# Dense block 0 made in memory of its own, beside the end of the last attention pass, with the routing exponential behind it

## The chip, the cores and the metric
The kernel runs on one core of one Trainium2 chip. Its time is the device time of one execution in microseconds (us), given as the median of several runs. The engines are TensorE (PE, matmuls; PEld are its weight loads), VectorE (DVE), ScalarE (ACT), GpSimd (POOL) and SyncE (SP, which here only issues transfers). Each runs its own list of instructions in order and waits on semaphores for the others.

## The reference
Input are 16 x 256 = 4096 tokens of 512 values. First comes a layer of attention over the 16 heads of each token, then a feed-forward layer:

```python
x = x + xattn(layernorm(x), ctx, ctx, ...)        # scores between the 16 heads of one token
x = x + ffn(layernorm(x), ...)

def ffn(z):                                       # E = 8 experts, F = 352, shared width 704
    scores = softmax(z @ gate_weight.T)
    topk_w, topk_idx = top_k(scores, 2)
    y = sum over the 2 experts: w * (silu(z @ gate.T) * (z @ up.T)) @ down.T
    sgu = z @ shared_gate_up.T
    return y + (silu(sgu[:, :704]) * sgu[:, 704:]) @ shared_down.T
```

## The kernel before
**Passes.** The tokens go in 16 blocks of 256. Attention is a loop of passes: pass i scores and attends block i, projects block i + 1 ahead, and does the rest of block i - 1 behind it (output projection `project_out`, residual and statistics `add_attended`, normalised rows `z`, their transposes `turn_z`, the routing logits `route` and `turn_logits`). Pass 15 (`NB - 1`) is written out and projects nothing ahead. What is left of block 15 is done behind it, the steps called with `NB`.

**Dense blocks.** The shared (dense) feed-forward part works on the same 16 blocks, which the text calls dense blocks 0 to 15. `gate_up(i, b, fs)` makes the gate and up products of six chunks f of 128 hidden units (the last has 64), one PSUM bank for each; 24 matmuls a chunk, 12 for the last. Every product is made of three fp16 matmuls, of a high and a low part. Then ScalarE makes the SiLU (`gate`), VectorE multiplies by the up half (`gate_times_up`), ScalarE rounds to the high part (`hidden_high`), VectorE makes the low part (`hidden_low`), and PE multiplies by the down weights (`down`, 36 matmuls: chunks 0 to 4 for both halves of the tokens, then chunk 5 for both). VectorE adds the result to `base` (`add_shared`). Each chunk passes between the engines four times. `sh_out` counts what VectorE finishes: six chunks and two halves, so 8 (`SH_STEPS`) a block.

**Around block 0.** Its weights are cut into high and low parts in pass 15: `shared_high` (ACT) and `shared_low` (DVE), four pieces each, once `find_scale` has a power of two for them. PE runs `gate_up(0, ...)` in three places between the last steps of block 15, since its banks are free by then. Before the first of them it waits for all four `shared_low` and for the two scales `wsd_scaled` and `wd_scaled`, because their input lies in a bank that `gate_up` writes. `gate_act` (the SiLUs, three buffers in turn) and `sh_t` (the hidden parts) lie in memory that the passes use until their last stores to HBM have landed. So ScalarE and VectorE turn to block 0 only when `x1`, `z` and the columns `zt` of block 15 are stored: VectorE waits for that, makes the routing maximum and difference (L1670, L1671), ScalarE the routing exponential (L1225), and only then `gate(0, 0)` (L1236) follows on ScalarE.

**SyncE's list.** It issues in this order: the stores of block 15, after their landing the eight loads of the routed experts' gate and up weights (`load_expert`, L668), a store that clears the slot table (L676), the columns of dense block 2 (`next_columns`, L607), the store of base 0 (L662), after that store has landed the load of base 2 (L611), the columns of block 3, and so on; the down weights of the experts (L679) stand behind the columns of block 4.

**Routing.** Behind `add_shared(0)` VectorE picks the top two experts of all tokens (L1725 to L1742), PE ranks them between two parts of `gate_up(1, ...)`, and behind `add_shared(1)` VectorE works out the slots (L1750 to L1770). In blocks 2 and 3 it also finds the largest expert weight in 16 reductions (`largest`, L1705). GpSimd scatters the token numbers to their slots beside blocks 2 to 8. Then come the routed experts, 71 slots of 128 rows, and the last six dense blocks with the sum of all parts.

The waits of PE that order `down(0)`:

```python
for step in ("LT", "Z0", "Z1"):
    wait_drained(pe, step, NB)
down(0, 0)
```

## Time and profile before

| | us |
|---|---|
| median of 3 runs | 1449.7 (1448.55 to 1450.1) |
| the profiled execution, device time | 1446.31 |
| its span in the profile | 1444.6 |
| PE busy in the span | 1340.1 (93%) |
| DVE busy | 884.4 (61%) |
| ACT busy | 674.4 (47%) |
| mean granted clock of PE | 0.98 |

The time runs about 1.7 us over the span in the profiled execution. In a timeline a row is a group of like instructions: its start, its length, engine, line of the kernel, what it writes and reads, the count, and in brackets the idle time before it with what ended it. The clock that PE is granted has two levels, 1.00 (2.4 GHz) and 0.50 (1.2 GHz).

### The profile page before, as it was taken

To read this page: it belongs to the slowest core of one execution; us is meant where nothing else is said; L and a number is where in the kernel's file an instruction comes from. 1 tells how busy PE (TensorE), PEld (TensorE's weight loads), DVE (VectorE), ACT (ScalarE), POOL (GpSimd) and SP (SyncE) were. 2 spreads that over 40 slices of the span, in tenths; PEclk is the share of its full clock that TensorE was granted. 3 is DMA by queue.
4 is the path that set the end of the run, shared out by engine and by line. 5 is a ranking of instruction groups with operands and counts; after the bars stand their busy time and mean duration, and the time that the engine had idled before them with its cause. 6 is when DMAs were issued, how large, how long until landed. Compare 5 with 4: busy or idle time off the path is not lost.

```text
span 1444.6 us, 34230 instructions
## 1 busy us (share of the span) xinstructions
PE 1340.1 (93%) x11411; PEld 1005.0 (70%) x11412; DVE 884.4 (61%) x1952; ACT 674.4 (47%) x1500; POOL 372.7 (26%) x480
## 2 busy tenths in 40 slices
PE   4799999999999997788999999999999999999997
PEld 4688788888888885656767756666666666657675
DVE  6888888888888888667855532232232232224566
ACT  6276667777676776431444423333333333332121
POOL 4322222222222220004566011111111111104554
PEclk9899999999999998899999999999999999999999
DMA  5556766776767658497734622222222222227996
GB/s 197 134 141 190 198 196 185 204 204 199 189 185 202 185 138 270 129 350 134 113 53 83 148 95 81 80 86 80 81 85 82 80 86 81 81 72 235 315 312 225
DMA packets 212740, 223.20 MB, mean 155 GB/s; under 512 B 84693, under 2 KB 142109, under 8 KB 212334
## 3 DMA queue, kind: packets, MB, share of 16 engines
q1 hardware_dynamic: 193608, 178.62, 43.5%
q0 software_dynamic: 12880, 35.47, 8.1%
q10 hardware_dynamic: 6198, 8.40, 2.0%
q8 instruction: 32, 0.52, 0.2%
q14 instruction: 22, 0.18, 0.1%
HBM read 129.30 MB, written 67.96 MB: 137 GB/s over the span
## 4 chain that ended last, share of the span: by engine, by line
PE 80%; DVE 11%; issue 2%; ACT 2%; DMA 2%; SPq 1%; POOL 0%; DVEq 0%; POOLq 0%; ACTq 0%
PE psum_b L726 44%; PE psum_a L726 30%; PE psum_b L1016 2%; PE psum_b L1038 2%; DVE z_parts L1472 1%; DVE k_scale L1394 1%; DVE d_m L1705 1%; PE psum_b L752 1%; SPq L488 1%; DVE wdn L1791 1%; DMA heads<-in_wk_t 1%; DVE gate_act L1680 1%; ACT z_parts L1120 1%; DMA wgu_in<-base_rows 1%; PE psum_b L784 0%
## 5 line engine op out<-in xcount | busy, mean ns | idle before, releaser
L726 PE MATMUL psum_a<-wgu,zg_t 128*128 x1704 | 267.7, 314 | 2.1 <-DVE zg_t L1802 1.7
L726 PEld LDWEIGHTS psum_a<-wgu,zg_t 128*128 128x128 f16 x1704 | 166.1, 98 | 90.2 <-issue 10.3
L726 PE MATMUL psum_a<-zt_in,wsgu 128*128 128x256 f16 x1536 | 170.6, 273 | 1.0 <-ACT y_sb L1306 0.8
L2025 POOL DMA_INDIRECT zg<-z_rows,gather_ix x71 | 67.2, 946 | 402.9 <-DVE gather_ix L1798 395.8
L726 PEld LDWEIGHTS psum_a<-zt_in,wsgu 128*128 128x128 f16 x1536 | 148.8, 98 | 24.9 <-issue 6.5
L1807 DVE SCALAR_TENSOR_TENSOR silu<-psum_a,w_scale,silu 128x352 f32<-128x352 f32 x71 | 41.5, 584 | 191.1 <-ACT silu L1293 191.1
L726 PE MATMUL psum_b<-wdn,act_t 128*128 (+1 forms) x639 | 149.6, 379 | 1.6 <-DVE act_t L1814 1.6
L726 PE MATMUL psum_b<-wsdn,sh_t 128*128 128x512 f16 (+1 forms) x576 | 134.4, 388 | 14.9 <-DVE sh_t L1686 14.4
L1912 POOL TENSOR_SCALAR var_eps<-mv 128x1 f32<-128x1 f32 x64 | 28.4, 443 | 429.7 <-DVE mv L1371 289.9
L1293 ACT ACTIVATE silu<-psum_a,w_scale 128x352 f32<-128x352 f32 x71 | 39.4, 554 | 202.4 <-PE psum_a L726 202.4
L726 PEld LDWEIGHTS psum_b<-wsdn,sh_t 128*128 128x128 f16 (+1 forms) x576 | 54.6, 99 | 88.9 <-issue 18.3
L1084 ACT ACTIVATE at_raw<-psum_a 32x128 f32<-32x128 f32 x384 | 103.2, 269 | 28.0 <-PE psum_a L726 23.5
L726 PE MATMUL psum_b<-cx_t,wk 128*128 128x256 f32 x768 | 102.9, 292 | 12.8 <-DVE k_scale L1414 6.5
L1236 ACT ACTIVATE gate_act<-psum_a,ws_scale 128x256 f32<-128x256 f32 x64 | 30.0, 470 | 175.1 <-PE psum_a L726 174.6
L1813 DVE TENSOR_TENSOR act_t<-psum_b,act_t 128x256 f16<-128x256 f32 x71 | 30.2, 425 | 129.6 <-ACT act_t L1084 129.6
L726 PEld LDWEIGHTS psum_b<-cx_t,wk 128*128 128x128 f32 x768 | 96.7, 196 | 16.9 <-DVE k_scale L1414 6.6
L726 PEld LDWEIGHTS psum_b<-wdn,act_t 128*128 128x128 f16 (+1 forms) x639 | 62.4, 98 | 61.6 <-issue 1.9
L1084 ACT ACTIVATE spread_t<-paired 32x512 f32<-32x512 f32 x128 | 90.2, 705 | 31.8 <-DVE paired L1458 30.6
L726 PE MATMUL psum_b<-wo,at_t 128*128 128x512 f32 x384 | 100.3, 415 | 0.0
L726 PE MATMUL psum_b<-xn_t,wq 128*128 128x256 f32 x768 | 97.5, 287 | 0.0
L1306 ACT ACTIVATE y_sb<-psum_b,wd_scale 128x512 f32<-128x512 f32 x71 | 48.8, 688 | 102.1 <-PE psum_b L726 102.1
L726 PEld LDWEIGHTS psum_b<-xn_t,wq 128*128 128x128 f32 x768 | 94.3, 194 | 0.7
(247 smaller groups left out, 2346.8 us busy)
## 6 DMA issues: line engine op xcount, KB each, us to landing
expert_rows<-y_sb SPq DMA_DIRECT2D x71, 256.0 KB, 2.0
k_st<-k_parts SPq DMA_DIRECT2D x192, 64.0 KB, 2.0
q_st<-q_parts SPq DMA_DIRECT2D x180, 64.0 KB, 2.0
wgu_in<-in_wgu_t SPq DMA_DIRECT2D x8, 1408.0 KB, 16.5
x_sb<-in_x SPq DMA_DIRECT2D x16, 512.0 KB, 5.5
cx_in<-in_ctx_t SPq DMA_DIRECT2D x16, 512.0 KB, 8.8
x_res<-in_x SPq DMA_DIRECT2D x16, 512.0 KB, 6.3
value_rows<-heads SPq DMA_DIRECT2D x16, 512.0 KB, 3.3
```

Of the source, the lines that this page charges most:

```text
L488: sp.dma_start(dst[HD * n:HD * (n + 1), :, KC * l:KC * (l + 1), :].rearrange("p j h g -> p j (h g)"), parts[HD * l:HD * (l + 1), part].rea ...
L726: return nc.tensor.matmul(o, l, r, start=start, stop=stop)
L1016: last = nc.tensor.transpose(t_bank[:, kc * P:(kc + 1) * P], zg[:, b, kc * P:(kc + 1) * P], ident[:, :])
L1038: last = nc.tensor.transpose(a_bank[0:fn, f * P:(f + 1) * P], silu[:, b, f0:f0 + fn], ident[:, :])
L1084: return nc.scalar.activation(o, i_, ACT.Copy)
L1236: nc.scalar.activation(gate_act[at:at + fn, f % GB, :], sh_bank(f)[0:fn, 0:BT], ACT.Silu, scale=ws_scale[0:fn, 3:4]).then_inc(silu_ready, 1)
L1293: nc.scalar.activation(silu[:, b, :], psum_a[:, 2 * b * BANK:2 * b * BANK + F], ACT.Silu, scale=w_scale[:, 3:4]).then_inc(g_silu, 1)
L1306: nc.scalar.activation(y_sb[:, b, :], d_bank[:, :], ACT.Copy, scale=wd_scale[:, 5:6]).then_inc(d_out, 1)
L1807: V.scalar_tensor_tensor(out=silu[:, b, :], in0=psum_a[:, (2 * b + 1) * BANK:(2 * b + 1) * BANK + F], scalar=w_scale[:, 4:5], in1=silu[:, ...
L1813: V.tensor_tensor(act_t[:, b, LO, 0:2 * P], psum_b[1][:, 0:2 * P], act_t[:, b, HI, 0:2 * P], ALU.subtract)
L1912: link(G.tensor_scalar_add(var_eps[:, col:col + 1], mv[:, col, 1:2], EPS))
L2025: pool.indirect_dma_start(out=zg[:, b, :], out_offset=None, in_=z_d[:, :], in_offset=bass.IndirectOffsetOnAxis(ap=gather_ix[:, b:b + 1], a ...
```

## The change
- `gates_of_first` (three gate buffers) and `hidden_of_first` (all hidden parts of one block) are placed in `wdn_in`, slots 2 to 6, where the last expert's gate and up weights land later. `gates_and_hidden(i)` gives these for block 0 and `gate_act`, `sh_t` for all others.
- SyncE waits in front of the eighth expert load for `sh_out` 8, that is for the whole of dense block 0.
- ScalarE in pass 15: `weights_out(0)`, two `shared_high`, `weights_out(1)`, two `shared_high`, instead of four `shared_high` and then both `weights_out`.
- VectorE in pass 15: the scales `wsd_scale` and `wd_scale` are found behind the fourth `shared_low`, not ahead of the first.
- ScalarE and VectorE behind pass 15: the steps of block 0 are put between those of block 15, in an order written out by hand; the wait for the stores, the routing maximum, the difference and the exponential come behind them.

```diff
+        gates_of_first = wdn_in[:, 2:4, :].rearrange("p e d -> p (e d)")[:, 0:GB * BT].rearrange("p (f t) -> p f t", f=GB)
+        hidden_of_first = wdn_in[:, 4:7, :].rearrange("p e d -> p (e d)").bitcast(F16).rearrange("p (h f t) -> p h f t", h=2, f=len(FS_CH))
+
+        def gates_and_hidden(i):
+            return (gates_of_first, hidden_of_first) if isinstance(i, int) and i == 0 else (gate_act, sh_t)
@@ SyncE
             def load_expert(e):
+                if e == E - 1:
+                    sp.wait_ge(sh_out, SH_STEPS)
+                    settle(sp)
@@ ScalarE, body
                 if isinstance(i, int) and i == NB - 1:
+                    weights_out(0, i)
                     act.wait_ge(ws_loaded, 48)
                     act.wait_ge(ws_scaled, 1)
-                    shared_high(range(KC))
-                weights_out(0, i)
-                weights_out(1, i)
+                    shared_high(range(2))
+                    weights_out(1, i)
+                    shared_high(range(2, KC))
...
@@ ScalarE, behind body(NB - 1)
             attended_out(NB)
             down_weights_high()
+            gate(0, 0)
+            gate(0, 1)
+            hidden_high(0, 0)
+            hidden_high(0, 1)
+            gate(0, 2)
+            gate(0, 3)
             z_out(NB)
             z_high(NB, 1)
+            hidden_high(0, 2)
+            hidden_high(0, 3)
+            gate(0, 4)
+            hidden_high(0, 4)
+            gate(0, 5)
+            hidden_high(0, 5)
             act.wait_ge(r_shift, 1)
             nc.scalar.activation(d_s[:, :, :], d_s[:, :, :], ACT.Exp).then_inc(r_exp, 1)
-            for f in range(len(FS_CH)):
-                gate(0, f)
-                if f > 0:
-                    hidden_high(0, f - 1)
-            hidden_high(0, len(FS_CH) - 1)
             gates(1, lambda f: None)
@@ VectorE, body
                 if isinstance(i, int) and i == NB - 1:
-                    find_scale(wsd_scale, psum_b[0][:, P:2 * P])
...
-                    find_scale(wd_scale, psum_b[0][:, 2 * P:3 * P])
-                    dve.sem_inc(wd_scaled, 1)
                     shared_low(0)
                     shared_low(1)
...
                 if isinstance(i, int) and i == NB - 1:
                     shared_low(2)
                     shared_low(3)
+                    find_scale(wsd_scale, psum_b[0][:, P:2 * P])
...
+                    find_scale(wd_scale, psum_b[0][:, 2 * P:3 * P])
+                    dve.sem_inc(wd_scaled, 1)
                 if behind:
                     turned_logits_out(i)
@@ VectorE, behind body(NB - 1)
             normalise_out(NB)
+            for f in range(2):
+                gate_times_up(0, f)
+            for f in range(2):
+                hidden_low(0, f)
             z_low(NB, 0)
+            for f in range(2, 4):
+                gate_times_up(0, f)
             logits_out(NB)
             z_low(NB, 1)
+            for f in range(2, 4):
+                hidden_low(0, f)
             turned_logits_out(NB)
+            for f in range(4, 6):
+                gate_times_up(0, f)
+                hidden_low(0, f)
             wait_drained(dve, "LT", NB)
...
             V.tensor_tensor(d_s[:, :, :], tok_scores[:, :, :], d_m[:, :].unsqueeze(2).broadcast_to([P, NT, E]), ALU.subtract).then_inc(r_shift, 1)
-            shared_block(0, 0, 0, nothing)
+            dve.wait_ge(base_loaded[0], 16)
+            add_shared(0, 0)
             dve.wait_ge(r_exp, 1)
```

## Rows read from the trace of the kernel before

**Rows 1.** The page: busy time of each engine.

```profile
PE 1340.1 (93%) x11411; PEld 1005.0 (70%) x11412; DVE 884.4 (61%) x1952; ACT 674.4 (47%) x1500; POOL 372.7 (26%) x480
```

**Rows 2.** Stretches of 20 us: busy time of the engines, granted clock, DMA.

```profile
600.00:620.00 20.00, 12.67 (x110) 10.29 (x109) 7.90 (x19) 6.46 (x14) 2.96 (x12) 0.90 0.43 155
```

**Rows 3.** The chain that ended last, in order of time: start, length, what.

```profile
611.37 2.99 DMA z_columns<-z_parts
...
615.83 1.28 ACT L1236
...
617.63 0.49 DVE gate_act L1680
618.15 0.42 ACT sh_t L1084
618.60 0.44 DVE sh_t L1686
...
619.27 9.76 PE psum_b L726 x36
```

**Rows 4.** Timeline of the end of pass 15 and the first part of gate_up(0).

```profile
570.87 5.55 ACT L1137 ACTIVATE wsgu<-wsgu_in,ws_scale 128x1408 f16<-128x1408 f32 x4 [2.46 <-DMA wsgu_in<-in_wsgu_t]
...
576.33 5.40 ACT L1084 ACTIVATE spread_t<-paired 32x512 f32<-32x512 f32 x8
...
577.43 0.28 DVE L1463 TENSOR_REDUCE wsd_scale<-psum_b 128x1 f32<-128x128 f32 x1
...
579.89 3.28 DVE L1487 SCALAR_TENSOR_TENSOR wsgu<-wsgu_in,ws_scale,wsgu 128x1408 f16<-128x1408 f32 x2 [0.16 <-DVE wd_scale L1468]
...
583.83 1.08 PE L726 MATMUL psum_b<-z_t,wgate 128*32 128x256 f32 x8 [5.08 <-DVE z_parts L1472]
...
585.91 3.27 DVE L1487 SCALAR_TENSOR_TENSOR wsgu<-wsgu_in,ws_scale,wsgu 128x1408 f16<-128x1408 f32 x2
...
588.53 0.66 PE L726 MATMUL psum_b<-strip_sum,logits_t 128*128 128x8 f32 x4
...
589.44 5.40 PE L726 MATMUL psum_a<-zt_in,wsgu 128*128 128x256 f16 x48 [0.25 <-DVE wsgu L1487]
```

**Rows 5.** Timeline of block 15's last steps on VectorE.

```profile
603.88 0.55 DVE L1519 TENSOR_SCALAR z<-x,mv,rstd 128x512 f32<-128x512 f32 x1 [0.76 <-POOL rstd L1913]
...
611.98 0.17 DVE L1482 COPY tok_scores<-psum_b 128x16 f32<-128x16 f32 x1 [0.71 <-PE psum_b L726]
```

**Rows 6.** Stretches of 1 us, as in rows 2; the granted clock is third from last.

```profile
572.00:573.00 1.00, 0.27 (x2) 0.00 (x0) 0.90 (x4) 1.00 (x2) 0.79 (x2) 1.00 1.16 311
...
575.00:576.00 1.00, 0.00 (x0) 0.00 (x0) 0.85 (x3) 1.00 (x2) 0.07 (x1) 0.50 1.06 389
...
622.00:623.00 1.00, 1.00 (x4) 0.36 (x3) 0.63 (x2) 0.20 (x1) 0.00 (x0) 0.60 1.03 397
```

**Rows 7.** SyncE's timeline, and the time to landing of its L607 at 634.89.

```profile
614.49 16.94 SPq L668 DMA_DIRECT2D wgu_in<-in_wgu_t  x8
...
634.89 7.43 SPq L607 DMA_DIRECT2D zt_in<-z_columns  x1
...
DMA to landing us min/median/max: 13.5/13.5/13.5
```

**Rows 8.** Timeline: down(1) on PE; block 2's first product, and its last down matmuls.

```profile
643.62 8.04 PE L726 MATMUL psum_b<-wsdn,sh_t 128*128 128x512 f16 x36
...
660.14 0.48 DVE L1680 SCALAR_TENSOR_TENSOR gate_act<-psum_a,ws_scale,gate_act 128x256 f32<-128x256 f32 x1
...
673.72 7.26 PE L726 MATMUL psum_b<-wsdn,sh_t 128*128 128x512 f16 x24 [1.04 <-DVE sh_t L1686]
```

**Rows 9.** SyncE's columns of block 5, their time to landing, and block 5's start.

```profile
710.00 3.12 SPq L607 DMA_DIRECT2D zt_in<-z_columns  x1
...
DMA to landing us min/median/max: 12.8/12.8/12.8
...
729.03 10.65 PE L726 MATMUL psum_a<-zt_in,wsgu 128*128 128x256 f16 x96
```

More of the change, by code:

```diff
@@ L934, in down @@
                             for hp, wp in PARTS:
-                                last = mm(sh_bank(n + s), sh_t[0:fn, hp, f, s * P:(s + 1) * P], wsdn[0:fn, wp, f, :],
+                                last = mm(sh_bank(n + s), hidden[0:fn, hp, f, s * P:(s + 1) * P], wsdn[0:fn, wp, f, :],
                                           f == 0 and (hp, wp) == PARTS[0], f == n - 1 and (hp, wp) == PARTS[-1])
@@ L1169, in body @@
                 if isinstance(i, int) and i == NB - 1:
+                    weights_out(0, i)
                     act.wait_ge(ws_loaded, 48)
                     act.wait_ge(ws_scaled, 1)
-                    shared_high(range(KC))
-                weights_out(0, i)
-                weights_out(1, i)
+                    shared_high(range(2))
+                    weights_out(1, i)
+                    shared_high(range(2, KC))
+                else:
+                    weights_out(0, i)
+                    weights_out(1, i)
                 if behind:
@@ L1235, in gate @@
                 at = REST if f == LAST else 0
-                nc.scalar.activation(gate_act[at:at + fn, f % GB, :], sh_bank(f)[0:fn, 0:BT], ACT.Silu, scale=ws_scale[0:fn, 3:4]).then_inc(silu_ready, 1)
+                nc.scalar.activation(gates_and_hidden(i)[0][at:at + fn, f % GB, :], sh_bank(f)[0:fn, 0:BT], ACT.Silu, scale=ws_scale[0:fn, 3:4]).then_inc(silu_ready, 1)
             def hidden_high(i, f):
@@ L1240, in hidden_high @@
                 act.wait_ge(sh_raw, i * len(FS_CH) + (f + 1))
[L1241 removed]
+                gates, hidden = gates_and_hidden(i)
+                copy(hidden[0:fn, HI, f, :], gates[0:fn, f % GB, :]).then_inc(sh_high, 1)
             def gates(i, after):
@@ L1260, in weights_high16 @@
                                ACT.Copy, scale=w_scale[:, 2:3]).then_inc(w_high16, 1)
-            for f in range(len(FS_CH)):
-                gate(0, f)
-                if f > 0:
-                    hidden_high(0, f - 1)
-            hidden_high(0, len(FS_CH) - 1)
+            attended_out(NB)
+            down_weights_high()
+            gate(0, 0)
[4 more added lines that the diff above has]
+            gate(0, 3)
+            z_out(NB)
+            z_high(NB, 1)
+            hidden_high(0, 2)
[4 more added lines that the diff above has]
+            hidden_high(0, 5)
+            act.wait_ge(r_shift, 1)
+            nc.scalar.activation(d_s[:, :, :], d_s[:, :, :], ACT.Exp).then_inc(r_exp, 1)
             gates(1, lambda f: None)
@@ L1661, in _ @@
             normalise_out(NB)
-            z_low(NB, 0)
-            logits_out(NB)
-            z_low(NB, 1)
-            turned_logits_out(NB)
-            wait_drained(dve, "LT", NB)
-            dve.wait_ge(z_stored, 16 * (NB + 1))
-            dve.wait_ge(x1_stored, 16 * (NB + 1))
-            dve.wait_ge(zt_stored, 16 * NB)
-            link(V.tensor_reduce(out=d_m[:, :], in_=tok_scores[:, :, :], axis=X, op=ALU.max))
-            V.tensor_tensor(d_s[:, :, :], tok_scores[:, :, :], d_m[:, :].unsqueeze(2).broadcast_to([P, NT, E]), ALU.subtract).then_inc(r_shift, 1)
             def sh_bank(step):
@@ L1679, in gate_times_up @@
                 at, up = (REST, 0) if f == LAST else (0, BT)
-                V.scalar_tensor_tensor(out=gate_act[0:fn, f % GB, :], in0=sh_bank(f)[at:at + fn, up:up + BT], scalar=ws_scale[at:at + fn, 4:5],
-                                       in1=gate_act[at:at + fn, f % GB, :], op0=ALU.mult, op1=ALU.mult).then_inc(sh_raw, 1)
+                gates = gates_and_hidden(i)[0]
+                V.scalar_tensor_tensor(out=gates[0:fn, f % GB, :], in0=sh_bank(f)[at:at + fn, up:up + BT], scalar=ws_scale[at:at + fn, 4:5],
+                                       in1=gates[at:at + fn, f % GB, :], op0=ALU.mult, op1=ALU.mult).then_inc(sh_raw, 1)
             def hidden_low(i, f):
@@ L1721, in nothing @@
                 pass
-            shared_block(0, 0, 0, nothing)
+            for f in range(2):
+                gate_times_up(0, f)
+            for f in range(2):
+                hidden_low(0, f)
+            z_low(NB, 0)
+            for f in range(2, 4):
+                gate_times_up(0, f)
+            logits_out(NB)
+            z_low(NB, 1)
+            for f in range(2, 4):
+                hidden_low(0, f)
+            turned_logits_out(NB)
+            for f in range(4, 6):
+                gate_times_up(0, f)
+                hidden_low(0, f)
+            wait_drained(dve, "LT", NB)
+            dve.wait_ge(z_stored, 16 * (NB + 1))
+            dve.wait_ge(x1_stored, 16 * (NB + 1))
+            dve.wait_ge(zt_stored, 16 * NB)
+            link(V.tensor_reduce(out=d_m[:, :], in_=tok_scores[:, :, :], axis=X, op=ALU.max))
+            V.tensor_tensor(d_s[:, :, :], tok_scores[:, :, :], d_m[:, :].unsqueeze(2).broadcast_to([P, NT, E]), ALU.subtract).then_inc(r_shift, 1)
+            dve.wait_ge(base_loaded[0], 16)
+            add_shared(0, 0)
             dve.wait_ge(r_exp, 1)
```

15 lines of the change are left out of this document (5 added, 10 removed).

## The prediction

> **What bounds the kernel now.** The busy line of the page comes first: PE works 93% of the span [rows 1], so time can only be won where PE stands still or runs at its lower clock. The stretches show where: from 600 to 620 us PE is busy 12.67 of 20 us at a granted clock of 0.90 [rows 2]. The chain of waits says why. PE's last matmul there ends at 611.9, and `down(0)` begins at 619.27, behind a line of single steps: the store of the columns lands (611.37 + 2.99), VectorE makes the routing maximum and difference and ScalarE the exponential (together 1.3 us), ScalarE loads its SiLU table (1.28), then SiLU, product, high part and low part of chunk 0 [rows 3]. That is 7.3 us of idle PE. The clock falls in it, and the 36 matmuls of `down(0)` take 9.76 us, where the 36 of `down(1)` take 8.04 [rows 3, 8]. So 9.0 us are to be had at most, if nothing else comes late. The timelines then tell what does.
>
> **Pass 15: the first part of gate_up(0) starts 1.45 us later.** Four `shared_high` take 5.55 us and eight copies of `weights_out` 5.40; the order is new and the sum is not. ScalarE can begin with `weights_out(0)` at 570.2, when VectorE has turned the pairs, and not at 570.87 when the weights land, so it comes to the columns of z some 0.65 us earlier. VectorE, without the two scales, has its first two `shared_low` done at 580.8 and waits there for ScalarE. `z_low(0)`, which lets PE's `route` go at 583.83, moves up by 0.8, and so do the last two `shared_low`, from 589.18 to 588.35. But the two scales now stand behind these: from 577.43 to 579.89 they take 2.3 us with their handoff left out. PE waits for both, so `gate_up(0)` starts at 588.35 + 2.3 + 0.25 = 590.9 where it started at 589.44 [rows 4]. From there to 611.9 PE had no gap, so this 1.45 us passes through to all of PE's steps.
>
> **Behind pass 15: ScalarE and VectorE.** What is added ahead of `z_low` costs PE nothing as long as it fits. VectorE ends z at 604.43 + 1.45 = 605.9 [rows 5], makes two products (0.9 us), waits for ScalarE's high parts and ends two low parts at 607.8; each handoff is as in rows 3. ScalarE then makes two SiLUs (1.0) and comes to z's first transpose at 608.15, where PE gave it at 608.0. `z_low(0)` ends at 610.0, and PE reaches `route` only at 611.0, so 1.0 us is left over; without that cover each us on VectorE is a us on PE. The columns are issued at 612.8, 1.45 later than before. The last transposed logits are out at 612.15 + 1.45 = 613.6, and PE, which waits for nothing later, starts `down(0)` at 613.9. Chunks 0 to 3 are ready by then (low part 3 ends at 613.6), chunk 4 at 615.4, where PE wants it at 616.5, chunk 5 at 616.8, where PE wants it past 620. With 0.3 us of idle time before it the clock has no reason to fall, so `down(0)` takes 8.0 and ends at 621.9 instead of 629.03: **7.1 us earlier**, 5.4 from the start and 1.7 from the clock.
>
> **The routing steps.** Maximum, difference and exponential now run at 616.9 to 619.5, with a table load for the exponential that was not there, and a second one back to SiLU. VectorE asks for the exponential only behind `add_shared(0)`, at 622.7, so 3.2 us cover them, and 1.28 us a load is all that rows 3 show: the SiLU starts at 617.12, the moment the load ends. The Trainium skill (ScalarE: Activation LUTs, What ACT_TABLE_LOAD costs) speaks against a change that goes from one set to another and back: it counts a drain beside the load, about 2.66 us a switch. This trace does not show the drain as lost time; by the page the exponential would be done at 620.9, which is still covered, with 1.8 us left; a loss from it is one of the small ones in the rest below. From `add_shared(0)` to the ranks everything keeps its distance to PE, so block 1 ends 7.1 us earlier too, at 644.5.
>
> **SyncE's list takes some of it back.** The expert loads start when the columns have landed, so they start 1.45 us later, at 615.9. The wait added in front of the eighth is met at 622.6 by `add_shared(0)`, and SyncE comes to it at 629.4, since the issues take 16.94 us in all [rows 7]; cost nothing, 6.8 us to spare. Behind the eight stand the columns of block 2. They were issued at 634.89 and landed 13.5 later, at 648.4 [rows 7], where PE asked for them at 651.6. Now they land at 649.85, and PE asks at 644.5. PE is idle for 5.4 us, and after such a gap the clock is down: it was so by 575, 2.7 us after PE fell idle at 572.3, and from 619.27 it took until 622.6 to rise [rows 3, 6]. I take 1.9 us lost to it. Chunk 0 of block 2 (24 of 96 matmuls of 10.65, [rows 9]) is done at 649.9 + 2.65 + 1.9 = 654.5, its product starts at 655.1. Before it was at 660.14 [rows 8], when VectorE came free from the slots; now that is at 653.0. From this product to the low part of chunk 4 VectorE was busy for 13.5 us without a pause, most of it `largest`. Now it also waits some 1.0 us for chunks 1 and 2, and the low part is there at 669.7, 4.0 earlier than the 673.7 before. The 24 matmuls behind it took 7.26, at a lower clock at first; PE, busy since 649.9, does them in 24/36 of 8.04 = 5.4 [rows 8]. So block 2 ends at 675.1 against 681.0: **5.9 us earlier**.
>
> **Later.** All that follows on PE, VectorE and ScalarE hangs on the block before it and keeps its length. Only transfers that don't move up can stop it. The nearest is the columns of block 5: issued at 710.00 behind a slow store, landed 12.8 later at 722.8, wanted at 729.03 [rows 9], now at 723.1. It just fits, even if SyncE's list does not move at all. Block 4's down weights stand behind the end of `gate_up(2)`, which stays where it was (666.5 for 666.1).
>
> **Sum.** -7.1 (start and clock of `down(0)`, with the 1.45 paid) + 1.2 (what block 2's late columns cost, less the clock saved in its `down`) = -5.9 us. The profiled execution took 1446.31 and would take 1440.4. It lies 3.4 us under the median of the runs shown, so the median is to be 1449.7 - 5.9 = 1443.8.
>
> **Bounds.** The clock in the wait of pass 15 is not shown: PE is idle from 589.2 to 590.9, 1.7 us, longer if its `attend` moves up with `route`. A gap of 0.25 us there left the clock up [rows 4], one of 2.7 us did not [rows 6]. The cost is 0 or 1.7 (some 3.4 us at half clock, as from 619.27 to 622.6 [rows 3, 6]). I take 0, as the gap is short of the 2.7. The half clock in block 2 costs between 0 and 2.4; I take 1.9, near what `down(0)` lost. Gates written to other memory cost the same, as size and type are the same.
>
> **Rivals.**
> 1. The clock falls in the wait of pass 15. All PE steps, the column store and the expert loads go 1.7 later: gain 4.2, time 1445.5. For it: PE had only just come up to full clock, and the gap is most of what was enough at 572. Against: it is shorter.
> 2. Block 2's columns don't hold: the transfers run faster or PE's clock stays up. Then VectorE's own chain decides, 653.2 for the first product and 667.9 for low part 4; gain 7.8, time 1441.9. Against: the eight expert loads stand ahead of the columns in either kernel, and they start later now.
> 3. Transfers cap the gain later: GpSimd's scatters start 7 us earlier and meet SyncE's base stores and columns, which then land no earlier or later, in blocks 4 to 6. Gain 1 to 3, time 1447.7. For it: block 5's columns have 0.3 us left.
> 4. Slower: the same list, but block 5's columns land more than 6.2 us later than now, past 729.0. From there each us is a loss; at 732 the time is 1449.7 + 3 = 1452.7, with a cold clock behind it. It would need the base store ahead of them, already slow, to become slower by a quarter.
> 5. The change doesn't do it: VectorE's inserted steps run over their 1.0 us cover, `route` and so `down(0)` start late by as much as is won, and PE still waits for low parts. Gain near 0, time 1449.5.
>
> **How the numbers follow.** Forecast 0.44; rival 1 0.22; rival 2 0.09; rival 3 0.10; rival 4 0.06; rival 5 0.05; the rest, 0.04, is a small loss spread over what is not seen. A change under 0.2% (2.9 us) can't be told from none here. Faster by more: forecast, rivals 1 and 2 and a third of rival 3 and some of the rest, 0.79. Slower by more: rival 4 and a little, 0.07. The range goes from rival 2 with 0.9 us to spare, 1441.0, to the slow end of rival 3, 1448.4.
>
> **What would show it.** In the profile after: the first matmuls of `gate_up(0)` about 1.5 us later and idle time before them that ends with the scale `wd_scale`; no gap over 0.5 us before `down(0)`, which takes 8.0 us; the exponential done before `add_shared(0)`; a gap of some 5 us before block 2, ended by the columns' landing; block 2's down without a half clock. The prediction is wrong if PE waits for low parts in `down(0)`, if block 2 starts without a gap, or if block 5 starts less than 5 us earlier.

## The result, and the profile after

| | before | after |
|---|---|---|
| median of 16 runs each on one chip, us | 1449.7 (1446.28 to 1465.34) | 1445.13 (1441.74 to 1452.17) |
| the profiled execution, us | 1446.31 | 1443.51 |
| its span, us | 1444.6 | 1441.8 |
| mean granted clock | 0.980 | 0.983 |

The ratio of after to before is 0.9963 (0.9945 to 0.9981): faster by 0.37%, 4.6 us by the medians; predicted was 5.9. The interval reaches from 2.8 to 8.0 us, so the forecast of 5.9 lies inside it, and the 1.3 us between 5.9 and 4.6 aren't told apart from nothing. The order of events came as predicted. The two profiled executions differ by 2.8 us (1446.31 to 1443.51; predicted was 1440.4); the one of the kernel before is as fast as the fastest of its 16 (1446.28).

The busy line of the page, for [rows 1], has hardly changed, as the work is the same:

```profile
PE 1341.0 (93%) x11411; PEld 1007.7 (70%) x11412; DVE 884.6 (61%) x1952; ACT 676.2 (47%) x1502; POOL 372.9 (26%) x480
```

Stretches of the changed kernel, columns as in rows 2 (granted clock third from last):

```profile
600.00:620.00 20.00, 19.73 (x144) 14.30 (x143) 11.69 (x26) 9.23 (x17) 2.96 (x12) 1.00 0.33 116
...
590.00:591.00 1.00, 0.00 (x0) 0.00 (x0) 0.88 (x7) 0.95 (x5) 0.00 (x0) 1.00 0.82 322
...
653.00:654.00 1.00, 1.00 (x7) 0.69 (x6) 0.45 (x2) 0.00 (x0) 0.31 (x2) 0.50 0.97 344
```

TensorE works 19.73 of the 20 us where it worked 12.67. The second row lies in the wait of pass 15: no matmul, and the clock at full. It had come up just before: the share granted is 0.50 in each us from 584 to 589 and 0.77 from 589 to 590. The third row is in block 2, at half clock. The timeline of pass 15, which answers to [rows 4]:

```profile
582.74 0.69 DVE L1492 SCALAR_TENSOR_TENSOR z_parts<-psum_b,z_parts 128x512 f16<-128x512 f32 x1 [1.80 <-ACT z_parts L1130]
...
588.76 0.28 DVE L1483 TENSOR_REDUCE wsd_scale<-psum_b 128x1 f32<-128x128 f32 x1
...
591.48 5.40 PE L735 MATMUL psum_a<-zt_in,wsgu 128*128 128x256 f16 x48 [1.71 <-DVEq L1617]
```

The scales stand behind the last `shared_low` and hold the first matmul for 1.71 us. DVEq L1617 is the signal that `wd_scale` is there. The timeline behind pass 15, for [rows 3, 5]:

```profile
614.02 0.17 DVE L1502 COPY tok_scores<-psum_b 128x16 f32<-128x16 f32 x1
...
614.25 8.05 PE L735 MATMUL psum_b<-wsdn,wdn_in 128*128 128x512 f16 x36 [0.27 <-DVE tok_scores L1502]
...
616.52 1.28 ACT L1286 ACT_TABLE_LOAD   x1
617.90 0.42 ACT L1286 ACTIVATE d_s<-d_s 128x256 f32<-128x256 f32 x1
618.34 1.28 ACT L1242 ACT_TABLE_LOAD   x1
...
621.76 1.41 DVE L1711 SCALAR_TENSOR_TENSOR base<-psum_b,wsd_scale,base 128x512 f32<-128x512 f32 x2 [3.89 <-PE psum_b L735]
```

`down(0)` starts 5.0 us earlier than in [rows 3], takes 8.05 for 9.76, and the exponential with both table loads fits between the last high part and `add_shared(0)`. SyncE's timeline, for [rows 7, 9]:

```profile
616.18 18.30 SPq L677 DMA_DIRECT2D wgu_in<-in_wgu_t  x8
634.52 1.87 SPq L685 DMA_DIRECT2D slot_tokens<-zero_id  x1
636.52 7.47 SPq L613 DMA_DIRECT2D zt_in<-z_columns  x1
```

TensorE's timeline from `down(1)` on, for [rows 8, 9]:

```profile
636.90 8.04 PE L735 MATMUL psum_b<-wsdn,sh_t 128*128 128x512 f16 x36
650.14 12.67 PE L735 MATMUL psum_a<-zt_in,wsgu 128*128 128x256 f16 x96 [5.21 <-DMA zt_in<-z_columns]
...
670.16 5.46 PE L735 MATMUL psum_b<-wsdn,sh_t 128*128 128x512 f16 x24 [0.82 <-DVE sh_t L1697]
675.54 10.65 PE L735 MATMUL psum_a<-zt_in,wsgu 128*128 128x256 f16 x96
...
723.71 10.65 PE L735 MATMUL psum_a<-zt_in,wsgu 128*128 128x256 f16 x96
...
747.20 10.65 PE L735 MATMUL psum_a<-zt_in,wsgu 128*128 128x256 f16 x96
```

`down(1)` is 6.7 us earlier; TensorE then waits 5.21 us for the columns of block 2. Block 5 starts at 723.71 for 729.03, 5.3 earlier. Block 6 starts 4.2 earlier and block 7 and those up to 9 start 3.1 earlier: in this execution ScalarE and VectorE fell behind once in each of blocks 5 and 6. A second execution of the same program (after_again, below) has no such loss, so the change doesn't cause it every time.

### The profile page after: what moved, and what is told of

The parts are those of the page before. It is cut to its first block, busy times and chain, and to the rows that moved or that the text cites. A ratio compares the mean times of both kernels' runs of the same rounds, so it can differ in the third digit from the quotient of the medians.

```text
span 1441.8 us, 34233 instructions
## 1 busy us (share of the span) xinstructions
PE 1341.0 (93%) x11411; PEld 1007.7 (70%) x11412; DVE 884.6 (61%) x1952; ACT 676.2 (47%) x1502; POOL 372.9 (26%) x480
## 4 chain that ended last, share of the span: by engine, by line
PE 77%; DVE 11%; ACT 3%; issue 3%; DMA 3%; SPq 1%; POOL 1%; another core or an unknown queue 0%; DVEq 0%; POOLq 0%; ACTq 0%
PE psum_b L735 42%; PE psum_a L735 29%; PE psum_b L1026 2%; PE psum_b L1048 2%; DVE z_parts L1492 1%; SPq L677 1%; DVE k_scale L1414 1%; PE psum_b L761 1%; DMA zt_in<-z_columns 1%; DVE d_m L1716 1%; DVE wdn L1824 1%; DMA wgu_in<-expert_rows,pos_ix 1%; DVE gate_act L1690 1%; DMA heads<-in_wk_t 1%; ACT z_parts L1130 1%
## 5 line engine op out<-in xcount | busy, mean ns | idle before, releaser
L735 PE MATMUL psum_b<-wsdn,sh_t 128*128 128x512 f16 x540 | 122.5, 379 | 6.1 <-DVE sh_t L1697 5.5
L735 PEld LDWEIGHTS psum_b<-wsdn,sh_t 128*128 128x128 f16 x540 | 50.2, 97 | 73.1 <-DVE sh_t L1697 11.3
```

The source lines that it names most:

```text
L735: return nc.tensor.matmul(o, l, r, start=start, stop=stop)
```

## The experiments

Each was run beside the kernel before, and the ratios are to the kernel before on the same chip. The chips differ, so times taken on two of them are compared by their ratios:

| chip | kernel before, us (runs) | experiments |
|---|---|---|
| A | 1447.89 (18) | exp_behind (11 runs), scales_in_gaps (6), columns_first (7), both_moves (6) |
| B | 1452.77 (35) | after_again (12), warm_pe (12), largest_behind (12), columns_free (12) |
| C | 1457.85 (17) | before_half (6), after_half (4), free_half (5), experts_wait (12) |

The changed kernel as it stands ran on B, but not on A and C. Where an expectation gives a time, it is counted from runs on an earlier chip, so what can be compared is its difference.

**exp_behind.** Half of the change alone: in the kernel before, the routing maximum, difference and exponential go behind the gates of block 0; the memory stays. ScalarE's part (VectorE's is left out here):

```diff
-            act.wait_ge(r_shift, 1)
-            nc.scalar.activation(d_s[...], d_s[...], ACT.Exp).then_inc(r_exp, 1)
+            wait_drained(act, "LT", NB)      # and the stores of block 15
...
+            act.wait_ge(r_shift, 1)          # behind hidden_high(0, 5)
+            nc.scalar.activation(d_s[...], d_s[...], ACT.Exp).then_inc(r_exp, 1)
```

> The kernel before, with one part of the change: the routing maximum, difference and exponential stand behind the gates of dense block 0, but these stay in gate_act and sh_t, so ScalarE waits itself until x1, z and the columns of block 15 have landed. My theory: the landing (614.5 in the profile of before) is the larger part of the wait, the routing steps only 1.3 us, with the table load of 1.28 us at most hidden too. Then down(0) starts 1.3 to 2.6 us earlier (616.7 to 618.0), its first matmuls still run at half clock, and the time falls by 1 to 3 us. The rival, that the exponential in front of the gates was what counted and the memory nothing: down(0) starts near 614 and the time falls by 5 us or more, as with the whole change.

Measured 1447.99 us, ratio 1.0001 (0.9993 to 1.001). Its timeline at `down(0)`:

```profile
614.93 1.28 ACT L1238 ACT_TABLE_LOAD   x1 [5.51 <-DMA z_columns<-z_parts]
...
618.48 10.66 PE L726 MATMUL psum_b<-wsdn,sh_t 128*128 128x512 f16 x36 [5.78 <-DVE sh_t L1688]
```

Here `gate_up(0)` ran 0.75 us late by chance, so `down(0)`, 0.8 earlier on the clock, is 1.5 earlier against the work ahead of it. But it takes 10.66 us for 36 matmuls where [rows 3] have 9.76. The half clock lasts from 617 to 623.8 here, of which `down(0)` runs 5.3 us, and from 616 to 622.8 in the kernel before, of which it runs 3.5: it starts earlier into a stretch that ends later. By the end of block 2 the gain is 0.2. So my theory of 1 to 3 us did not hold, and the rival of 5 us or more even less: the new order without the memory is worth nothing. The other half, the memory with the exponential left in front, was not run; so the gain needs the memory, and how much of it the memory brings alone is open.

**scales_in_gaps.** The changed kernel, with the two scales moved into gaps in which VectorE waits: `wsd_scale` behind the second `shared_low`, `wd_scale` behind `z_low(0)`.

```diff
                     shared_low(1)
+                    find_scale(wsd_scale, ...)
...                  z_low(i, 0)
+                    find_scale(wd_scale, ...)
...                  shared_low(3)
-                    find_scale(wsd_scale, ...)
-                    find_scale(wd_scale, ...)
```

> The changed kernel, with the two scales of pass 15 found in VectorE's idle time: wsd_scale behind the second shared_low, where it waits 1.8 us for ScalarE, wd_scale between z_low(0) and logits_out, where it waits 1.2 us for PE. My theory, that the place of the scales delays gate_up(0) and all of PE behind it: gate_up(0) starts at 589.8 instead of 591.5, everything behind it moves up by 1.7 us, the expert loads with it, so that block 2 starts at 648.4; time 1.7 us less than the changed kernel, about 1443.4. The rival, that this wait is hidden by something later (block 15's attention output, z): down(0) still starts at 614.2 and the time stays.

Measured 1440.77, ratio 0.9956 (0.9942 to 0.9971). TensorE's timeline:

```profile
589.83 5.50 PE L735 MATMUL psum_a<-zt_in,wsgu 128*128 128x256 f16 x48
...
612.68 8.05 PE L735 MATMUL psum_b<-wsdn,wdn_in 128*128 128x512 f16 x36 [0.27 <-DVE tok_scores L1502]
...
673.46 10.65 PE L735 MATMUL psum_a<-zt_in,wsgu 128*128 128x256 f16 x96
```

The wait of pass 15 is gone; against the trace of the changed kernel, `down(0)` starts 1.6 us and block 3 2.1 us earlier. In the traces this confirms the term of 1.45 us as a cost of the change that needn't be paid. The times don't show it by themselves: the ratio to the kernel before is 0.9956 here and 0.9963 (0.9945 to 0.9981) for the changed kernel on another chip.

**columns_first and both_moves.** The columns of block 2 are issued ahead of the expert loads, in the changed kernel and in scales_in_gaps.

```diff
+            next_columns(0, 0)
             for e in range(E):
                 load_expert(e)
...
-                next_columns(i, i % 2)
+                if i > 0:
+                    next_columns(i, i % 2)
```

> The changed kernel, with the columns of block 2 issued ahead of the eight expert loads instead of behind them. My theory, that their landing behind the experts costs the 5.2 us gap and the cold clock in front of block 2: the gap is gone, gate_up(2) starts at about 644.9 instead of 650.1 and runs at full clock, the first product of block 2 comes when VectorE is free of the slots (653.4), the low part of chunk 4 at about 668. Block 2 then ends at 673.3 to 675, since PE may again run cold in its down: 0.5 to 2.3 us less than the changed kernel, time 1443 to 1444.5. The rival, that VectorE's own work sets block 2's end in any case: the gap goes but block 2 ends at 675.5 as now, time as the changed kernel. A second rival, that the expert loads, 1.3 us later, come too late for the reductions: VectorE waits at 653 for their landing and block 2 ends later than 675.5.

> The changed kernel with both: columns of block 2 ahead of the expert loads, scales in VectorE's gaps. If each of the two waits is on the path of its own, the gains add: 2.2 to 4 us under the changed kernel, 1441.1 to 1442.9. If block 2 is bound by VectorE alone, moving PE up by 1.7 us still moves VectorE's routing steps up, so 1.7. If both hang on the same wait, no more than the larger one.

Measured 1442.8, ratio 0.9965 (0.9952 to 0.9977), and 1438.82, ratio 0.994 (0.9925 to 0.9955). TensorE's timeline in columns_first:

```profile
592.88 8.00 PE L737 MATMUL psum_a<-zt_in,wsgu 128*128 128x256 f16 x48 [1.56 <-DVEq L1619]
...
648.84 10.65 PE L737 MATMUL psum_a<-zt_in,wsgu 128*128 128x256 f16 x96
...
670.96 8.29 PE L737 MATMUL psum_b<-wsdn,sh_t 128*128 128x512 f16 x24 [1.69 <-DVE sh_t L1699]
679.18 10.65 PE L737 MATMUL psum_a<-zt_in,wsgu 128*128 128x256 f16 x96
...
837.28 9.66 PE L737 MATMUL psum_b<-wsdn,sh_t 128*128 128x512 f16 x36 [5.68 <-DVE gather_ix L1833]
```

Two stretches of 1 us of the same trace, in the wait of pass 15 and behind it:

```profile
591.00:592.00 1.00, 0.32 (x2) 0.22 (x2) 0.86 (x8) 0.96 (x4) 0.00 (x0) 0.50 1.02 412
...
595.00:596.00 1.00, 1.00 (x6) 0.72 (x5) 0.93 (x3) 0.96 (x3) 0.00 (x0) 0.50 0.00 0
```

The 5.2 us gap has gone: block 2 starts right behind block 1. But TensorE then waits for VectorE in `down(2)` (1.48, 1.43 and 1.69 us), the clock falls, and the last 24 matmuls take 8.29 for 5.46. From the start of block 1 (626.21) to the end of block 2 it is 52.97 us, in the changed kernel 53.31 (622.23 to 675.54). In the kernel before it was 51.95 (628.96 to 680.91). So the late columns cost 1.4 us (1.2 predicted), and without them 1.0 is still lost: they cover VectorE's own chain. My theory of 0.5 to 2.3 us under the changed kernel is not borne out, the first rival is. Rival 2 of the prediction (columns that don't hold, a gain of 7.8) would not have paid what it promised either. Its first product is right (31.2 us behind the start of block 1, for 31.3). From there to the low part of chunk 4 it had 14.7 us where the trace has 13.5, as in the kernel before (660.14 to 673.7, [rows 8]). And it left out the clock, which costs 2.8 in the last 24 matmuls.

In the wait of pass 15 the clock is not up at all: 0.50 in each us from 584 to 598, so the first 48 matmuls take 8.00 us for 5.40. The last row of the first view shows another wait, in front of `down(9)`. This profiled execution is the slowest of the seven (1452.27; median 1442.8), with both of these losses in it.

**after_again.** The changed kernel once more, on another chip.

> The changed kernel once more, beside the others of this call on the same chip. It shows what differs between executions of the same program. My theory of the 2.2 us that its first profile lost in blocks 5 and 6 (SiLU of a chunk 1.7 us late with PE long done): it is chance, not the change. Then here block 5 to block 8 take 22.4 us each, as in the kernel before. The rival, that GpSimd's scatters, which start 7 us earlier, now disturb these blocks: the same loss in blocks 5 and 6 again.

Measured 1449.44 against 1452.77 before, ratio 0.9971 (0.9949 to 0.9994). The chip is slower and its runs spread more than those of chip A. TensorE's timeline:

```profile
593.12 7.07 PE L735 MATMUL psum_a<-zt_in,wsgu 128*128 128x256 f16 x48 [1.46 <-DVEq L1617]
...
729.02 10.65 PE L735 MATMUL psum_a<-zt_in,wsgu 128*128 128x256 f16 x96
...
836.52 9.73 PE L735 MATMUL psum_b<-wsdn,sh_t 128*128 128x512 f16 x36 [3.30 <-DVE gather_ix L1831]
```

A wait of 1.46 us, shorter than the 1.71 above, and the half clock of rival 1, but not as rival 1 has it. The clock is full in the wait and when the matmuls start (1.00 from 591 to 594); it falls some 1.3 us behind their start (0.70 from 594 to 595) and is at half until 597.8. Blocks 5 to 8 take 22.39 us each, as before. `down(9)` is late by 3.30 us, as in columns_first by 5.68, each time with "<-DVE gather_ix" and with 9.7 us for 8.05 behind it. No wait of the kernel before ends so, and this one leads on.

**warm_pe.** both_moves with 18 unread matmuls of 512 columns in the waits of `down(2)`.

```diff
+                            if isinstance(i, int) and i == 2 and s == 0 and f in (2, 3, 4):
+                                sh_free(i, n + 1)
+                                for _ in range(6):
+                                    mm(sh_bank(n + 1), hidden[:, HI, 0, 0:P], wsdn[:, HI, 0, :], True, True)
```

> The kernel with both moves, and in addition 18 matmuls of 512 columns that nobody reads, six in front of each of the waits for chunks 2, 3 and 4 in down(2), where PE stands idle for 1.4 to 1.7 us each and the last 24 matmuls then take 8.34 us. My theory, that the early columns brought only 0.3 us because PE, now early, stands in front of VectorE and loses its clock: with the idle time filled the clock stays up, the last 24 take 5.4 to 5.5, block 2 ends 2.8 us earlier than with both moves (53.0 us behind the end of down(0) become 50.2) and the time falls by 2.8. The rival, that the early columns lose elsewhere, by slower reductions beside the transfers: the last 24 still begin at the same distance, but low part 4 itself is late, and the filling brings nothing or costs up to 1.3 us a wait.

Measured 1452.09, ratio 1.0003 (0.9982 to 1.0023). TensorE's timeline:

```profile
665.30 5.46 PE L737 MATMUL psum_b<-wsdn,sh_t 128*128 128x512 f16 x24 [0.39 <-DVE sh_t L1705]
...
828.15 9.94 PE L737 MATMUL psum_b<-wsdn,sh_t 128*128 128x512 f16 x36 [5.14 <-DVE gather_ix L1839]
```

The mechanism holds: with TensorE kept busy the 24 matmuls take 5.46 for 8.34 in both_moves, and block 2 ends 50.15 us after block 1 starts instead of 53.02. The time does not fall by 2.8 us, as I expected: some 160 us later `down(9)` waits 5.14 us for `gather_ix` and then takes 9.94 for 8.05, which is more than was gained. The trace shows no more than that. It is of the fastest of the twelve runs (1444.71; median 1452.09), and both_moves did not run on this chip, so where the typical run loses all that both moves had won isn't shown.

**largest_behind and columns_free.** both_moves with the reductions for the largest weight taken out from between VectorE's products and low parts in blocks 2 and 3 and put behind them (ten behind, six beside); and that with SyncE issuing each block's columns before it waits for the store of a base.

```diff
-                shared_block(i, i % 2, i // 2, lambda f: [largest(next(units)) for _ in range(2 if f % 3 == 2 else 1)])
+            for i, beside, behind_ in ((2, 0, 6), (3, 1, 4)):
+                gated_hidden(i, lambda f: [largest(next(units)) for _ in range(beside)])
...
+                for _ in range(behind_):
+                    largest(next(units))
```

> The kernel with both moves, and the 16 reductions of the expert weights placed where PE doesn't wait for VectorE: none beside the chunks of block 2 and six behind its last low part, one beside each chunk of block 3 and four behind it (8 and 8 between the chunks before). My theory: block 2 takes 22.6 us as the later blocks do instead of 30.4, block 3 22.6 instead of 23.4, so 8.6 us are to be had there. But SyncE's list doesn't move up with it: the columns of block 5 are issued behind the landing of base 2, 706.8 with both moves, and land 12 us later at 718.8, where block 5 would start at 712.8. So I expect block 5 to wait some 4 to 6 us and the whole gain to be 2.5 to 4.5 us under both moves. The rival, that the list follows the blocks: no gap in front of block 5, gain 8 us or more.

> As largest_behind, and SyncE issues the columns of the next block before it waits for the landing of a base store (store of base i, columns of block i + 3, then the wait and the load of base i + 2). My theory, that this wait caps what PE can gain: the gap in front of block 5 goes, and the time is 7 to 9 us under both moves, near 1430 to 1432. The rival, that the columns' own transfer among the scatters and the staged down weights is what is slow: a gap remains in front of block 5 or 6, and the time is that of largest_behind.

Measured 1447.75, ratio 0.9969 (0.9947 to 0.9992), and 1442.45, ratio 0.9939 (0.9919 to 0.9959). TensorE's timeline in largest_behind:

```profile
704.84 10.42 PE L737 MATMUL psum_b<-wsdn,sh_t 128*128 128x512 f16 x36 [4.20 <-DVEq L1828]
716.80 10.65 PE L737 MATMUL psum_a<-zt_in,wsgu 128*128 128x256 f16 x96 [1.54 <-DMA zt_in<-z_columns]
...
830.71 10.63 PE L737 MATMUL psum_b<-wsdn,sh_t 128*128 128x512 f16 x36 [9.70 <-DVE gather_ix L1840]
```

The same in columns_free:

```profile
717.71 10.65 PE L749 MATMUL psum_a<-zt_in,wsgu 128*128 128x256 f16 x96
...
827.89 9.87 PE L749 MATMUL psum_b<-wsdn,sh_t 128*128 128x512 f16 x36 [5.97 <-DVE gather_ix L1852]
```

Blocks 2 and 3 now run without a hole (22.4 and 22.6 us), and the lead is given back in two places. One is `down(4)`, with 4.20 and 4.86 us of idle time and 10.4 us for 8.04 behind it. It waits for a scale of VectorE that stands behind the cutting of the staged down weights, and there ScalarE waited 3.51 and 4.17 us for their transfer. The other is `down(9)`. Block 5's columns do come late once the lead is large (1.54 us), and don't with the freer list of columns_free.

My sizes were wrong in both. I expected a gap of 4 to 6 us before block 5 and got 1.54, did not see the wait in `down(4)`, and of the 2.5 to 4.5 and 7 to 9 us under both moves nothing is to be seen in the ratios (0.9969 and 0.9939 for 0.994). On the same chip columns_free is 5.3 us under largest_behind by the medians, but this isn't the gap of block 5: in the traces block 5 starts 0.9 us later in columns_free, and the wait in `down(9)` is 3.7 shorter. Whether the freer list or chance shortened it isn't shown.

**What holds down(9).** VectorE makes `gather_ix` from the token ids that GpSimd has scattered to their slots with 64 indirect transfers, and that are loaded back. GpSimd's load and VectorE's first step behind it, from the timeline of the changed kernel:

```profile
806.90 0.62 POOL L2050 DMA_DIRECT2D zero_id<-slot_tokens  x1 [14.80 <-DMA slot_tokens<-tok_ix,pos_ix]
...
816.30 0.21 DVE L1859 CAST id_rows<-zero_id 71x128 f32<-71x128 int32 x1
```

The same of after_again:

```profile
816.71 0.62 POOL L2050 DMA_DIRECT2D zero_id<-slot_tokens  x1 [15.88 <-DMA slot_tokens<-tok_ix,pos_ix]
...
823.04 0.22 DVE L1859 CAST id_rows<-zero_id 71x128 f32<-71x128 int32 x1 [3.52 <-DMA zero_id<-slot_tokens]
```

The load in both_moves:

```profile
803.00 0.62 POOL L2054 DMA_DIRECT2D zero_id<-slot_tokens  x1 [11.00 <-DMA slot_tokens<-tok_ix,pos_ix]
```

The line from the known slots to this load takes 147 to 160 us (653.29 to 806.9, 656.60 to 816.7, 651.33 to 803.0; in the kernel before 660.03 to 811.5, in exp_behind 660.14 to 807.6), and it differs between executions by more than the gain in question. In the four executions traced on chip B it takes 156 to 160 us, in those on chip A 147 to 159. Where `id_rows` waited, it came 4.1 to 10.0 us behind this load. It came 9.4 us behind it in after and 8.0 in the kernel before (811.47 to 819.44), so neither has sure room for a line that is a few us longer. Three kernels test whether it is the second bound.

**before_half, after_half, free_half.** The kernel before, the changed one and columns_free, with the first of each token's two picks scattered and the second left out; half of the slot table is not written.

```diff
-                for pick in range(TOPK):
+                for pick in range(1):
```

> The kernel before, in which GpSimd scatters only the first of each token's two picks (32 indirect transfers for 64), so half of the slot table is left unwritten and the output is not the reference's. My theory: GpSimd's line from the known slots to the token ids is a second bound, but in the kernel before it ends with little to spare and holds nothing in most executions. So the ids are there about 35 us earlier than the 811.5 of the kernel before, no step of TensorE moves by over 1 us, the time is that of the kernel before less 0 to 3 us (less for those executions in which the ids came late), and the spread of its times is smaller. Rival: the scatters slow SyncE's transfers or the engines beside them as well; then blocks 2 to 9 get shorter and the time falls by over 4 us.

> The changed kernel with the same half of the scatters (half of the slot table is left unwritten, the output is not the reference's). Theory: what the change gains in front of the slots stays, with no late ids in any execution: 5 to 6 us under before_half, at a narrower spread than the changed kernel against the kernel before (4.6 us under it by the medians, some executions over it). Down(9) starts without idle time that ends with gather_ix. Rival: the spread and the missing us come from the clock in the wait of pass 15 alone; then the distance to before_half stays at 3 to 5 us and the spread as it was.

> columns_free (all moves together) with the same half of the scatters (half of the slot table is left unwritten, the output is not the reference's). Theory: the 5.97 us of idle time before down(9), which ended with gather_ix, is gone, and what was won behind the slots reaches the end of the kernel: 13 to 15 us under before_half, where columns_free lay 10.3 under the kernel before; the 4.9 us that TensorE waits in down(4) for its staged weights stay. Rival: the ids are not the cause, the idle time turns up again before another step of blocks 9 or of the routed part (the routed weights, the gathered rows), and the time is 10 to 11 us under before_half, as columns_free against the kernel before.

On this chip the kernel before took 1457.85 (1447.94 to 1461.94, 17 runs).

| | median, us | range | ratio to before |
|---|---|---|---|
| before_half | 1448.79 | 1446.9 to 1454.27 | 0.994 (0.9925 to 0.9955) |
| after_half | 1441.86 | 1440.81 to 1443.96 | 0.9893 (0.9875 to 0.9911) |
| free_half | 1430.74 | 1429.85 to 1432.93 | 0.9823 (0.9807 to 0.984) |

GpSimd's load of the ids in before_half:

```profile
749.84 0.62 POOL L2017 DMA_DIRECT2D zero_id<-slot_tokens  x1 [5.25 <-DMA slot_tokens<-tok_ix,pos_ix]
```

And two rows of its TensorE, `down(9)` and the last 24 matmuls of `down(14)`:

```profile
835.42 8.05 PE L726 MATMUL psum_b<-wsdn,sh_t 128*128 128x512 f16 x36
...
1415.71 7.76 PE L726 MATMUL psum_b<-wsdn,sh_t 128*128 128x512 f16 x24 [4.32 <-DVE sh_t L1686]
```

The same place in the kernel before:

```profile
1410.08 5.46 PE L726 MATMUL psum_b<-wsdn,sh_t 128*128 128x512 f16 x24 [0.91 <-DVE sh_t L1686]
```

In after_half:

```profile
745.29 0.62 POOL L2050 DMA_DIRECT2D zero_id<-slot_tokens  x1 [5.87 <-DMA slot_tokens<-tok_ix,pos_ix]
```

TensorE's timeline in free_half:

```profile
704.88 2.76 PE L749 MATMUL psum_b<-wsdn,sh_t 128*128 128x512 f16 x12 [1.07 <-DVEq L1840]
...
818.62 8.05 PE L749 MATMUL psum_b<-wsdn,sh_t 128*128 128x512 f16 x36
```

The ids are there 62 us earlier (35 expected), and no `down(9)` waits in these three traces. With this bound away the change is worth 6.9 us by the medians of six and four runs (1448.79 to 1441.86), and all moves 18.1; I expected 5 to 6 and 13 to 15. The ranges of before_half and after_half don't overlap, but so few runs can't tell 6.9 from 5.9. The theory is right in its kind and was too small in its sizes: I expected 0 to 3 us between before and before_half, and there are 9.1 on this chip. The rival's reading, that the scatters slow the blocks, finds no support in the profile of before_half: from block 5 to `down(9)` it is 104.2 us (731.22 to 835.42), as in the kernel before (729.03 to 833.23). In free_half I was wrong to expect the wait in `down(4)` to stay: it is 1.07 us for 4.86, so the scatters seem to be part of what made the staged weights late (the two traces are of different chips). That the missing 9.1 us of the kernel before were spent in `down(9)` is inferred: no trace of one of its longer executions on this chip was taken.

There is a second place where an execution can lose as much, and half the scatters don't remove it. The profiled execution of before_half is the slowest of its six (1454.27; median 1448.79), and `down(9)` is not late in it. It lost 5.7 us in `down(14)`: VectorE waited 3.03 us for gathered rows of the experts, TensorE 4.32 us for VectorE where it waited 0.91 in the kernel before, and the clock fell, so that 24 matmuls took 7.76 us for 5.46. So a long execution needs no late ids, and the spread of the kernel before has at least this rival cause.

**experts_wait.** The changed kernel, with the new wait of SyncE in front of the first expert load.

```diff
-                if e == E - 1:
+                if e == 0:
                     sp.wait_ge(sh_out, SH_STEPS)
```

> The changed kernel with the wait for sh_out 8 in front of the first expert load instead of the eighth. Theory (SyncE's list is in order, and the columns of block 2 stand behind the loads): the eight loads start at about 623 for 616.2, the columns of block 2 land 6.5 to 7 us later, near 656.5, TensorE is idle for 12 us before gate_up(2), and block 2 ends near 682.5 for 675.5: 6 to 7 us over the changed kernel, 1 to 2 over the kernel before, which shows what the place of this wait is worth. Rival: the loads move at their own pace once they are alone on the queues, or the columns go by other queues beside them; then the columns land less than 3 us later and the time is within 3 us of the changed kernel.

Measured 1457.95 against 1457.85, ratio 1.0016 (0.9996 to 1.0037): nothing is gained over the kernel before. The changed kernel itself did not run on this chip, so its gain here is not known and the loss is read from the traces. SyncE's timeline in the profiled execution (1450.09 us, the fastest of the twelve):

```profile
624.45 18.24 SPq L677 DMA_DIRECT2D wgu_in<-in_wgu_t  x8
```

And TensorE's:

```profile
658.37 12.52 PE L735 MATMUL psum_a<-zt_in,wsgu 128*128 128x256 f16 x96 [12.35 <-DMA zt_in<-z_columns]
```

The loads start 8.3 us later, the columns follow them (TensorE gets them 8.2 later), and block 2 ends at 685.14, 9.6 later than in the changed kernel, of which 1.1 was there at `gate_up(0)` already. That is more than the 6 to 7 us expected. SyncE's list works as a fixed line of transfers; the eighth load is a place where the wait is free, since SyncE comes to it at 630.1 (629.4 predicted) and it is met at 623.2.

## Why the prediction was right, and where not

- **Start of gate_up(0)**: predicted 590.9 with idle time ending with `wd_scale`; 591.48 with 1.71 us. The scales took 2.3 us as counted (588.76 to 591.07); of the 0.6 more, 0.4 is `shared_low`, which ended at 588.76 for 588.35, and the rest the handoff. The 0.4 has its cause on ScalarE: it was to come to the columns of z some 0.65 us earlier and came 0.13 earlier (581.62 for 581.75), since it began `weights_out(0)` at 570.45 and not at 570.2, and the four pieces in the new order took 11.2 us for 10.9.
- **ScalarE and VectorE behind pass 15**: predicted that the inserted steps fit ahead of `route`; `z_low(0)` at 609.75, `route` at 611.58. Right. `down(0)` at 614.25 for 613.9, with 0.27 idle for 0.3, and 8.05 us for 8.0.
- **The routing exponential**: done at 618.3, asked for at 623.1. The trace shows ScalarE's table load as 1.28 us, 0.02 behind its last high part, and the exponential 0.1 behind the end of the load, just when VectorE's difference was there (617.87). The Trainium skill (ScalarE: Activation LUTs, What ACT_TABLE_LOAD costs) counts a drain beside the load. The trace doesn't agree: no time of that size is lost at either of the two loads, nor in [rows 3], where the load ends at 617.11 and the SiLU starts at 617.12.
- **Columns of block 2**: gap 5.4 predicted, 5.21 measured; half clock 1.9 predicted, 2.02 measured (12.67 for 10.65). End of block 2: 675.1 and 675.54; 5.4 us gained for 5.9. In terms of the sum, 6.7 for 7.1 in front of block 1 and a cost of 1.4 for 1.2 in block 2.
- **Block 5**: columns in time, 5.3 us earlier. Rival 4 did not come. Of rival 3's kind there is 1.3 us in after_again, where `down(4)` waits for its staged weights (703.01 to 729.02 for 704.29 to 729.03), and nothing in after.
- **The clock in the wait of pass 15** was to cost 0 or 1.7 us and taken as 0, as the gap is short of 2.7. This size was luck for the execution profiled. Of the five traced executions with this wait, after (1.71 us) and experts_wait (1.72) lost nothing, after_again (1.46) and after_half (1.88) lost 1.7, and columns_first (1.56) 2.6. The nine traced without it lost 0.1 at most. The mechanism of rival 1, a clock that falls in the wait, is in none of the five: where 1.7 was lost the clock was full all through the wait and fell about 1 us behind its end, and in columns_first it had not yet come up. The length of the gap doesn't decide between them. What it costs in a typical run isn't known, so it can be a part of the 1.3 us between 5.9 and 4.6.
- **The bound not seen**: GpSimd's line of scatters up to block 9. The prediction looked for transfers that cap the gain in blocks 4 to 6 (rival 3) and missed this one, as no wait of the profile before ended with it: the load is issued 8.0 us ahead of its reader there, within the 4.1 to 10.0 that such a load took elsewhere. The change brings the slots forward too (653.3 for 660.0), so its own gain need not be lost there: in after nothing is, in after_again 3.3 us and the clock behind them are. What an experiment gains behind the slots has no such help. The kernels with half the scatters, where the change is worth 6.9 us by the medians, are compatible with the 5.9; how the 4.6 splits between this bound, the clock, waits such as the one in `down(14)` and chance can't be told from these runs.

**The best version.** columns_free, at 0.9939 (0.9919 to 0.9959), beat the changed kernel on its own chip (1442.45 against 1449.44 for after_again). both_moves has 0.994 (0.9925 to 0.9955) and is not told apart from it by the ratios. The changed kernel did not run beside both_moves; columns_first did, with 1442.8 against 1438.82.

## What to carry to other kernels

When an idle stretch in front of an engine is removed, follow each in-order list (DMA queue, GpSimd) to the step at which it next meets that engine, however far off, and write down its slack: here the columns met TensorE one block on, and the scattered ids eight blocks on. A gain made ahead of the point from which such a list starts moves the list too; a gain behind it lasts only until the two meet. And where the times of a kernel spread by more than the gain, one profile shows one path: ask of each long line of transfers whether its slack in that profile is larger than the spread.

## Not expected of the hardware

- The clock can fall behind a gap and not in it. In after_again (gap 1.46 us) and after_half (1.88) it was full through the gap, fell about 1 us behind the next matmul's start and stayed at half for some 3 us; in after (1.71) and experts_wait (1.72) it held.
- A shorter gap can cost more: after 5.78 us idle 36 matmuls took 10.66 (exp_behind), after 7.33 us 9.76 (the kernel before).
- The landing of GpSimd's last indirect scatters holds the load behind it for 8.3 to 15.9 us with 64 of them and for 5.3 to 5.9 with 32.
- The kernel before on the chips A, B and C: 1447.9, 1452.8 and 1457.9 us, with half the scatters on C 1448.8.
